# A decoder's layer norms: the mean matmul reads two half sums added on VectorE instead of four chunks

## The reference

```
def _layernorm(x, axis=-1, eps=1e-05):
    m = jnp.mean(x, axis=axis, keepdims=True)
    v = jnp.var(x, axis=axis, keepdims=True)
    return (x - m) / jnp.sqrt(v + eps)

x = _layernorm(x + sparse attention(x))          # norm 0
x = _layernorm(x + wkv recurrence(x, ctx))       # norm 1
x = _layernorm(x + mixture of 16 experts(x))     # norm 2
x = _layernorm(x + causal attention(x))          # norm 3
x = _layernorm(x + cross attention(x, ctx))      # norm 4
x = _layernorm(x + swiglu FFN(x))                # norm 5, the output
```

## Time and profile before

| what | value |
|---|---|
| time, median of 3 runs | 2637.64 us (2634.35 to 2638.93) |
| the profiled execution | 2634.15 us, its span 2632.2 us |
| busy share of the span | PE 76%, DVE 70%, ACT 49%, POOL 36% |
| mean granted TensorE clock | 0.893 of full speed |
| norm 0, from PE's first matmul to the next block's first work | 440.87 to 477.14 us |

### The profile page before, as it was taken

The page is one execution under the profiler, slowest core; times in us unless marked ns, Lnnn a source line. Parts: engine busy times, 40 slices in busy tenths (PEclk is TensorE's granted clock), DMA queues, the critical chain, the costliest instruction groups (busy, mean ns, idle before and its releaser), DMA issues. The chain is left out here.

```text
span 2632.2 us, 33369 instructions
## 1 busy us (share of the span) xinstructions
PE 2009.7 (76%) x12104; PEld 1245.7 (47%) x12139; DVE 1850.9 (70%) x2514; ACT 1297.3 (49%) x2147; POOL 945.4 (36%) x547
## 2 busy tenths in 40 slices
PE   2888765025499999999956799988994776699985
PEld 1456642012376666666633566753542332244442
DVE  4249984986777888888843465554443997999976
ACT  0013322655386776776713232325554875466656
POOL 1014443213246777877725222224101000444330
PEclk8988877557699999999988899998997898899998
DMA  3225655001538999999951000002335330000001
GB/s 145 64 102 189 219 199 221 0 0 33 194 111 265 265 276 271 259 271 277 255 144 63 1 1 1 1 27 102 96 96 181 133 111 1 0 1 1 0 1 64
DMA packets 119668, 305.52 MB, mean 116 GB/s; under 512 B 29521, under 2 KB 49489, under 8 KB 115794
## 3 DMA queue, kind: packets, MB, share of 16 engines
q1 hardware_dynamic: 98450, 252.58, 26.3%
q0 software_dynamic: 21056, 50.84, 10.1%
HBM read 215.67 MB, written 88.77 MB: 116 GB/s over the span
## 5 line engine op out<-in xcount | busy, mean ns | idle before, releaser
L1330 PE MATMUL x_group<-x_xt,x_gu 128*128 128x256 f16 x2640 | 362.0, 275 | 33.4 <-DVE x_part L1441 17.9
L1441 DVE SCALAR_TENSOR_TENSOR x_part<-x_group,x_scale,x_part 128x256 f32<-128x256 f32 x660 | 286.5, 474 | 94.9 <-ACT x_part L1383 84.0
L1296 POOL TENSOR_TENSOR x_part<-x_part 128x512 f32<-128x512 f32 x165 | 236.0, 1430 | 169.5 <-DVE x_part L1441 168.7
L1330 PEld LDWEIGHTS x_group<-x_xt,x_gu 128*128 128x128 fp8e4 x2640 | 229.4, 98 | 140.6 <-issue 60.0
L1383 ACT ACTIVATE x_part<-x_group,x_scale 128x256 f32<-128x256 f32 x660 | 264.5, 472 | 10.8 <-PE x_group L1330 10.6
L2440 POOL TENSOR_TENSOR f_part<-f_part 128x1024 f32<-128x1024 f32 x44 | 120.5, 2738 | 187.6 <-DVE f_part L2467 187.6
L158 PE MATMUL mean_n<-residual,const_tables 128*128 128x512 f32 x160 | 78.7, 647 | 139.8 <-PEq L765 104.1
L1776 POOL TENSOR_TENSOR c_pt<-c_pt,const_tables 128x1024 f32<-128x1024 f32 x32 | 75.8, 2369 | 255.7 <-ACT c_pt L1750 255.7
L2338 PE MATMUL f_group<-f_x_hi,f_raw 128*128 128x512 f16 x352 | 138.7, 394 | 33.0 <-DVE f_part L2467 25.7
L1287 POOL DMA_INDIRECT mixed_rows<-x_y,moe_rows x94 | 150.1, 1597 | 32.0 <-issue 20.1
L1347 PE MATMUL x_y_ps<-x_d_hi,x_h_hi 128*128 128x512 f32 x330 | 157.8, 478 | 2.7 <-ACT x_y L1405 1.8
(11 more groups left out here) (332 smaller groups left out, 4993.2 us busy)
## 6 DMA issues: line engine op xcount, KB each, us to landing
x_d_hi<-down_hi SPq DMA_DIRECT2D x50, 768.0 KB
x_d_lo<-down_lo SPq DMA_DIRECT2D x50, 768.0 KB
x_gu<-codes_gu SPq DMA_DIRECT2D x50, 384.0 KB
p_w<-d_s SPq DMA_DIRECT2D x17, 768.0 KB, 7.7
down_hi<-p_hi SPq DMA_DIRECT2D x17, 768.0 KB, 3.9
down_lo<-p_lo SPq DMA_DIRECT2D x17, 768.0 KB, 6.3
aux<-ct SPq DMA_DIRECT2D x2, 4096.0 KB, 15.3
cross_values<-y_v_out SPq DMA_DIRECT2D x16, 512.0 KB, 2.8
```

Source lines behind the costliest of these rows:

```text
L1296: pool.tensor_tensor(x[:, 0, :, :], x[:, 0, :, :], x[:, 1, :, :], ALU.add).then_inc(summed, 1)
L1330: mm = pe.matmul(group_ps[s % 2][:, q, :], codes[:, q, col:col + P], xt[u][:, k, q, :], start=k == 0, stop=k == 1)
L1441: dve.scalar_tensor_tensor(x, group_ps[s % 2][:, 2 + q, :], scale[v][:, o, 2 + q:3 + q], x, ALU.mult, ALU.add).then_inc(ev_dve, 1)
```

## The change

In the halved norms a new DVE step `fold(t)` adds chunks 2 and 3 of the tile onto chunks 0 and 1 into a new buffer `sums` (two of them, [128, 2, 512] fp32 each), and `mean(t)` reads the two chunks of that buffer instead of the four of the tile. So there are 16 new DVE additions of 128x1024 in the program (4 norms by 4 tiles), and 32 fp32 matmuls fewer. A new semaphore `folded_x` makes `mean` wait for its fold; `fold(t)` for t of 2 and more waits until mean t-2 has read the buffer. Norms 2 and 3 are as they were.

```
+        sums = [sb(f"sums{i}", [P, C // 2, TT]) for i in range(2)] if halved else None
...
             def mean(t):
                 if t >= 2:
                     pe.wait_ge(centred_ready, base + t - 1)
-                for c in range(C):
-                    mm = pe.matmul(mean_ps[t % 2][:, :], g.const("mean"), tile(src, t)[:, c, :],
-                                   start=c == 0, stop=c == C - 1)
+                if halved:
+                    pe.wait_ge(folded_x, base_pairs + t + 1)
+                x, terms = (sums[t % 2], C // 2) if halved else (tile(src, t), C)
+                for c in range(terms):
+                    mm = pe.matmul(mean_ps[t % 2][:, :], g.const("mean"), x[:, c, :], start=c == 0, stop=c == terms - 1)
                 mm.then_inc(mean_ready, 1)
...
+            def fold(t):
+                if halved:
+                    if t >= 2:
+                        dve.wait_ge(mean_ready, base + t - 1)
+                    x = tile(src, t)
+                    dve.tensor_tensor(sums[t % 2][:, :, :], x[:, 0:2, :], x[:, 2:4, :], ALU.add).then_inc(folded_x, 1)
...
             fill(0)
+            fold(0)
+            fold(1)
             centre(0)
+            fold(2)
             centre(1)
+            fold(3)
             pair(0)
             centre(2)
             pair(1)
```

More of the change, by code:

```diff
@@ L139, in layer_norm @@
         base = NT * layer
-        mean_ready, centred_ready, squares_ready, var_ready, ln_ready, rs_ready, normed, paired = g.ln_sems
+        mean_ready, centred_ready, squares_ready, var_ready, ln_ready, rs_ready, normed, paired, folded_x = g.ln_sems
         halved = prepare_next is None
@@ L2567, in decoder @@
         g.ln_sems = [ctx.enter_context(nc.semaphore("ln_" + n)) for n in
-                     ("mean_ready", "centred_ready", "squares_ready", "var_ready", "ln_ready", "rs_ready", "normed", "paired")]
+                     ("mean_ready", "centred_ready", "squares_ready", "var_ready", "ln_ready", "rs_ready", "normed", "paired", "folded_x")]
         g.pairs = 0
```

## The result

| | changed kernel | kernel before |
|---|---|---|
| median, in the first comparison | 2641.48 us (10 runs, 2636.32 to 2644.82) | 2635.04 us (10 runs, 2632.84 to 2638.93) |
| ratio, first comparison | 1.0022, 95% interval 1.0013 to 1.0031 | |
| ratio, the same kernel run again later | 1.0009, interval 1.0000 to 1.0019 | |
| the profiled execution, its span | 2641.69 us, 2639.9 us | 2634.15 us, 2632.2 us |

So the change is slightly slower: 6.4 us by the medians of the first comparison (5.8 by its ratio), 1.7 us by the medians of the second (2.4 by its ratio), whose interval begins at no change at all. The forecast was +3.1 us and 2640.7, counted from a median of three runs, 2637.64; the ten runs of the kernel before in the first comparison have 2635.04.

The account below looks back on a forecast made before the run. PE's mean matmuls held a norm's front end up to its first Ln, ACT the rest. DVE path and fill +1.4, one norm's clock +1.7: +3.1 us on the median 2637.64, giving 2640.7 us; range 2634 to 2647.

Parts of the forecast that it names:

- The queue in place of the wait: Front end up to Ln 0: PE's wait goes, but folds 2 and 3 delay pair 0; gain 0.05 us in norm 0.
- rival 3: Folds 0, 2 and 3 on the path cost 2.29 us each, not 1.22: +16 us, 2653; chance 0.03.
- Rival 2: Front end: Ln 0 moves with the squares, not pair 0; 1.3 us a norm won, -3.7 us, 2634; chance 0.12.
- Two terms: Front end: var 0's start to Ln 0, 2.18 us; mean 0's last record to centre 0, 0.15 us.
- warm sum: DVE path and fill over four norms, clock as before: -0.05 - 0.10 + 0.06 + 1.44 = +1.4 us.
- The fill: Norm 4: fill 0 ahead of fold 0 loses mean 0's cover; +1.5 us, Ln 0 at 16.8, about +1.44 net.
- The clock: PE's hole before var 0: one chance in four per norm of cold var 0, +1.73 us; one norm, +1.7 us.
- rival 1: Mean 2 to var 0: clock drops in most norms, 1.73 us each, +8.3 us with the 1.4, 2646; chance 0.27.
- The size of the total: Whole program: +1.4 us for DVE path and fill, +1.7 for one norm's clock, +3.1 us in all.
- the part that I gave 0.22: Whole program slower by over 0.2% (5.3 us): 0.17 of rival 1, 0.03 of rival 3, and noise on the forecast.

Follow-up runs that it names:

- Experiment 1: Pair 0 put ahead of fold 3 on DVE, against the changed kernel: 2636.24 us, ratio 1.0002 to the kernel before.
- experiment 3: Fill 0 put behind folds 0 and 1 on DVE, against the changed kernel: 2639.75 us, ratio 1.0009 to the kernel before.
- experiment 6: Changed kernel with norm 4 left as before, without sums, folds or wait: 2638.68 us, ratio 1.0005 to the kernel before.
- experiment 8: Changed kernel with pair 0 ahead of fold 3 and fill 0 behind folds 0 and 1: 2633.6 us, ratio 0.9992 to the kernel before.
- experiment 2: Changed kernel with extra unused fp32 matmuls, one behind mean 1, two behind mean 2: 2635.42 us, ratio 1.0000 to the kernel before.
- experiment 4: Changed kernel folding only tiles 1 and 2, both ahead of centre 0, fill 0 behind them: 2631.97 us, ratio 0.9985 to the kernel before.
- experiment 9: Changed kernel with three buffers, folds 0 to 2 ahead of centre 0, then fill 0, mean 3 unfolded: 2626.48 us, ratio 0.9963 to the kernel before.

## Why the prediction was right, point by point

**The queue in place of the wait.** Right. The forecast had centre 0 at 5.2, pair 0 at 11.85, Ln 0 at 15.31 us with the clock up; measured 5.10, 11.78 and 15.07. Two smaller things went with it: ACT idled 0.89 us for a forecast 1.1, and the stretch from Ln 0 to the end of the last scale kept its length, 20.64 to 20.66 us in norms 0, 1 and 5 (before, 20.62 to 20.64), although var 3 ran cold in seven of the eight norms of the changed kernel's two profiles (3.43 to 3.78 us): the tail is ACT's. A fold costs 1.22 us, as pair does, and 1.14 from start to start in the chain; rival 3 is out. Rival 2 (Ln 0 follows the squares) failed where the forecast put it: pair 0 stood behind the folds, with ACT idle 0.89 us. Experiment 1 took fold 3 away from there, and Ln 0 did follow.

**Two terms were mis-sized.** I gave var 0 2.18 us up to Ln 0, from 454.05 and 456.23 in the earlier trace rows. In the changed kernel, where ACT waits, it is 2.02 (454.69 to 456.71). Before, Ln 0 wasn't waiting for var 0 but for ACT itself: it comes 3.34 us behind the start of square 1 in both profiles of before (12.02 and 15.36 in norm 0, 12.32 and 15.66 in the second), and again in experiment 1 (10.76 and 14.09). The other is the time from mean 0's last record to centre 0. I took 0.15 us and called it what remains of 2.18 after three steps of 0.43 and a record of 0.59; but that remainder is 0.30, so my working would have given centre 0 at 5.3. Measured are 3.82 us from PE's start to centre 0 (442.92 to 446.74), which leaves 0.08 behind the four cold records of 3.74. That 5.2 came out nearly right is luck. Together the two make the warm norm 0.24 us better than forecast. The warm sum is therefore not +1.4: the kernel with extra matmuls, warm throughout, had 144.8 us in its norms against 144.4 and 144.9, that is +0.1 against their mean and +0.4 against the first profile.

**The fill.** Right: fold 0 at +1.50 us; norm 4 was 37.3 to 37.7 us long when warm, 36.3 to 36.5 before, where +1.44 was forecast and the above 0.24 comes off.

**The clock.** Right in mechanism, and about right in frequency. Forecast were one chance in four per norm and 1.73 us each. Fifteen norms in four profiles have this hole of 2.42 us before var 0 (the changed kernel twice, experiments 3 and 6); var 0 was cold in five of them, at 1.35 to 1.65 us each. In the 24 norms of the six profiles with folds but a shorter hole (0.7 to 1.4 us), it was cold in none. The first profile had two such norms, the second one. So rival 1 describes what happened in some norms, not in most.

Which norms they are can be read from the first burst. The records of means 0 and 1 run from half clock into full clock, so the burst's length tells how late the clock came up. In the ten warm norms of the fifteen it is 5.08 to 5.88 us, in the five cold ones 6.06 to 6.38, without overlap. A late rise went with a clock that falls around the end of the hole of 2.42 us: by the windows it fell at 587.3 in norm 1, 0.1 us before var 0 began, and at 2205.2 in norm 4, 0.5 us behind its beginning. Experiment 1 had a burst of 6.28 us in norm 0:

```profile
445.60 6.28 PE L162 MATMUL mean_n<-sums_n,const_tables 128*128 128x512 f32 x8 [24.47 <-DVE sums_n L197]
```

and its var 0, behind 1.29 us of idle, was warm all the same; so were norm 1 of experiment 8, with a burst of 6.57 us and the same hole, and norms 1 and 4 of experiment 2, with bursts of 6.16 and 6.37 us and work in the hole. Behind a late burst, then, var 0 was cold in five norms of five with the hole of 2.42 us, and in none of four with a shorter one. This, more than experiment 2 by itself, shows that the hole is what costs the clock.

One piece of my evidence was weaker than I took it for. I let the tail of the earlier trace rows, with 2.82 us of idle ahead of var 3 and a clock that held, speak for the hole. In experiments 4 and 9 the tail has the same matmuls behind the same gaps of 1.80 and 2.82 us, and var 3 ran wholly or partly at half clock in six norms of eight. Norm 4 of experiment 4:

```profile
2207.30 1.98 PE L177 MATMUL var_n<-squares_n,const_tables 128*128 128x512 f32 x4 [1.80 <-DVE squares_n L204]
2212.10 3.64 PE L177 MATMUL var_n<-squares_n,const_tables 128*128 128x512 f32 x4 [2.81 <-DVE squares_n L204]
```

It costs nothing there, as Ln 3 isn't waiting for it. The one chance in four was thus partly luck.

The Trainium skill's page "TensorE: Matmul & The Clock Gate" warned of this in the section "A second HAM failure mode: psum-queue depth-cycling". The runs agree in kind; in degree they don't, as it struck 5 of 15 norms. That the same norm is warm in one run and cold in the next agrees with what the section "What's actually happening" says of a free-running monitor.

**The size of the total.** Two profiles of each kernel give 146.8 against 144.7 us for the norms, +2.1, where +3.1 was forecast. The ratios say +5.8 us (1.0022) and +2.4 us (1.0009). The second agrees with the norms; of the first, 3.7 us are in no part of the program that I can name. What speaks for chance is the 4.1 us by which equal code ahead of norm 0 differs from profile to profile; what stays open is why the first comparison's whole interval, 1.0013 to 1.0031, lies above the 1.0008 of the norms, as the intervals of experiments 1 and 8 lie above what their norms gained.

That the median of 2641.48 lies within 0.8 us of the forecast 2640.7 is luck. The forecast started from 2637.64, which is 2.6 us over the median of the ten runs of the kernel before; the measured distance was +6.4 by the medians for a forecast +3.1, and its parts were others: in the first profile about +0.4 for path and fill and +3.0 for two cold norms, where +1.4 and +1.7 were forecast. The first comparison (1.0022) lies just over the 0.2% that I called the least that can be told from no change, in the part that I gave 0.22, and the second (1.0009) well under it; with ten runs a side the intervals are only 0.09 to 0.10% to each side, so the 0.2% was too coarse.

## What to carry to other kernels

When work moves from one engine to another, look at where it lands in the receiving engine's list, and place it where that engine waits anyway. The four folds a norm, with folds 2 and 3 on the path ahead of pair 0, cost the norms some 2 us in all; three folds a norm in DVE's idle time ahead of the first centre (and mean 3 left as it was) saved 10. And a lighter TensorE isn't faster by itself: look at the holes that it gets, and at what runs behind them at half clock.

## What the runs showed of the hardware that was not expected

TensorE's clock fell in five norms around the 2.42 us of idle before var 0, with 1.01 to 1.32 us before mean 2 ahead of that; it stayed up in ten norms with the same 2.42 us and 1.51 to 1.89 us before mean 2, which is more idle time, and in the kernel before behind 1.80 and 2.82 us, where it fell in six norms of eight in experiments 4 and 9. The length of a gap alone doesn't tell which way it goes. What told the fifteen norms apart was how late the clock had come up in the burst before.

A mean 0 of eight records, some cold and some not, made the start of a norm vary from 5.45 to 6.71 us between norms of one profile (experiment 4). With four records, all cold or nearly so, it was 5.05 to 5.10 in all four norms of experiment 9, and less where the clock came up sooner (4.86 in norm 1 of experiment 1).
